# Seven block products in place of eight for the values of blocks 0 and 1, made between two down products

## The reference

```python
qkv = x @ w_qkv.T                                  # 512 -> 3 * 512
q, k, v = ...                                      # 16 heads of 32
q = q * cos + rotate_half(q) * sin                 # k likewise
scores = einsum('bhqd,bhkd->bhqk', q, k) * scale   # keep 0 <= q - k < 64
attn = softmax(scores); out = einsum('bhqk,bhkd->bhqd', attn, v)
x = layernorm(x + out @ w_out.T)
gate = silu((x @ w_gate) * s_gate); up = (x @ w_up) * s_up
x = layernorm(x + ((gate * up) @ w_down) * s_down)
```

## Time and profile before

| what | value |
| --- | --- |
| time, median of 3 runs | 1167.76 us (1167.47 to 1167.96) |
| time of the profiled execution | 1167.22 us |
| its span | 1165.4 us |
| busy: PE, DVE | 1154.4 us (99%), 985.7 us (85%) |
| busy: POOL, ACT | 587.9 us (50%), 584.5 us (50%) |
| granted PE clock, mean | 0.999 of full speed |

### The profile page before, as it was taken

How to read it: one execution, slowest core, us unless ns; L and a number is a source line. 1 busy time by engine, 2 the same in 40 slices (tenths; PEclk the granted TensorE clock), 3 DMA queues, 4 the chain that set the end, 5 groups by cost and what they waited for, 6 DMA issues and landing times.

```text
span 1165.4 us, 25537 instructions
## 1 busy us (share of the span) xinstructions
PE 1154.4 (99%) x8433; PEld 569.4 (49%) x8433; DVE 985.7 (85%) x2820; ACT 584.5 (50%) x1640; POOL 587.9 (50%) x563
## 2 busy tenths in 40 slices
PE   9999999999999999999999999999999999999997
PEld 4344446444464444644455444554445544464444
DVE  7899998898988989879998899897898988986434
ACT  3863883048820588105880159701686027950330
POOL 0775684256731667326671367613676236752330
PEclk9999999999999999999999999999999999999999
DMA  9999786356662665617656086561964527734000
GB/s 296 164 182 244 140 170 152 71 88 137 115 149 55 108 130 110 144 42 128 130 99 141 37 146 119 100 132 42 159 124 87 131 64 137 119 73 109 19 1 36
DMA packets 351933, 134.80 MB, mean 116 GB/s; under 512 B 309824, under 2 KB 332224, under 8 KB 351808
## 3 DMA queue, kind: packets, MB, share of 16 engines
q1 hardware_dynamic: 334832, 106.73, 49.2%
q0 software_dynamic: 10560, 17.30, 5.0%
q10 hardware_dynamic: 6416, 9.13, 2.1%
HBM read 32.19 MB, written 8.39 MB: 35 GB/s over the span
## 4 chain that ended last, share of the span: by engine, by line
PE 96%; ACT 1%; DVE 1%; issue 1%; POOL 0%; POOLq 0%
PE bank L835 61%; PE bank L1051 18%; PE bank L841 10%; PE bank L977 3%; PE bank L957 2%; PE bank L857 1%; ACT bank L1236 1%; PE bank L1073 1%; PE bank L866 0%; PE bank L1062 0%; ACT wu L1179 0%; DVE fuse L1364 0%; ACT fuse L1179 0%; PE bank L941 0%; DVE row_max L1536 0%
## 5 line engine op out<-in xcount | busy, mean ns | idle before, releaser
L835 PE MATMUL bank<-x1T,wg 128*128 128x512 f16 (+1 forms) x1032 | 242.5, 378 | 0.0
L835 PE MATMUL bank<-x1T,wu 128*128 128x512 f16 x1024 | 241.9, 379 | 0.0
L1236 ACT ACTIVATE bank<-bank,neg_max,qk_scale 128x128 f32<-128x128 f32 x512 | 220.7, 436 | 8.1 <-DVE neg_max L1549 6.2
L1051 PE MATMUL bank<-wd,fuse 128*128 128x512 f16 (+1 forms) x1056 | 222.7, 373 | 0.0
L653 POOL TENSOR_TENSOR fuse<-ffn_tmp,fuse 128x512 f16<-128x512 f32 x128 | 149.8, 1170 | 117.0 <-ACT fuse L1179 116.4
L735 POOL TENSOR_TENSOR fuse<-fuse 128x512 f16<-128x512 f32 x116 | 137.6, 1218 | 74.0 <-ACT fuse L1179 71.9
L1051 PEld LDWEIGHTS bank<-wd,fuse 128*128 128x128 f16 x1056 | 103.1, 98 | 116.6 <-DVE y L1604 0.2
L835 PEld LDWEIGHTS bank<-x1T,wu 128*128 128x128 f16 x1024 | 100.2, 98 | 120.6
L648 POOL TENSOR_TENSOR xT_sb<-probs,xT_sb 128x512 f16<-128x512 f32 x112 | 129.9, 1160 | 44.6 <-ACT xT_sb L1179 44.5
L835 PEld LDWEIGHTS bank<-x1T,wg 128*128 128x128 f16 x1032 | 96.4, 98 | 113.9 <-issue 4.0
L1189 ACT ACTIVATE ffn_tmp<-bank,tanh_scale 128x512 f32<-128x512 f32 x128 | 88.3, 690 | 99.5 <-PE bank L835 74.9
(11 more groups left out here) (234 smaller groups left out, 1624.6 us busy)
## 6 DMA issues: line engine op xcount, KB each, us to landing
v_cross<-v_own SPq DMA_DIRECT2D x64, 128.0 KB, 2.4
out<-x ACTq DMA_DIRECT2D x32, 256.0 KB, 2.0
xT_sb<-xT SPq DMA_DIRECT2D x30, 256.0 KB, 4.0
qkT<-x SPq DMA_DIRECT2D x28, 256.0 KB, 3.7
wg<-w_gate POOLq DMA_DIRECT2D x7, 1024.0 KB, 5.1
wu<-w_up POOLq DMA_DIRECT2D x7, 512.0 KB, 5.9
wqkv<-w_qkvT SPq DMA_DIRECT2D x8, 256.0 KB, 6.0
wg<-w_gate POOLq DMA_DIRECT2D x1, 2048.0 KB, 8.2
```

The costliest lines, as they stand in the source:

```text
L835: last = pe.matmul(dst, lhsT, rhs, start=(i == 0), stop=(i == len(pairs) - 1))
L1051: last = pe.matmul(dst[:, cols], fuse[:, s, z, rows], wd[:, s, cols], start=(s == 0 and z == 0), stop=(s == STEPS - 1 and z == 1))
L1236: last = act.activation(unit, unit, ACT.Exp, bias=neg_max[:, s % 2, h // 3, h % 3:h % 3 + 1], scale=qk_scale[:, 2:3], accum_out=row_sum[:, ...
```

## The change

The values of blocks 0 and 1 of the next tile are made by `project_v_pair` with seven block products of 128 rows by 256 columns in place of eight, and PE runs it between down products 2 and 3. The sums of weights for it are made by POOL in each body (`add_v_weights`), after it has inverted the first layer norm's deviations; POOL's reload of the gate and up columns, which it overwrites, moves behind the values. ACT keeps the first product (`keep_v_first`) between the stores of rows 0 and 1. DVE sums the products (`sum_v`, seven additions of 256 columns) ahead of `finish_y(f, 2)` and keeps the low halves (`split_v_pair`). The rope sums of blocks 0 and 1 go from DVE to POOL. `carry_keys` and `start_tables` move ahead of `start_y(f, 1)`.

```diff
+            def add_v_weights(a):
+                low_left, low_right, high_left, high_right = v_quarters()
+                wait(proj_done, pool, a - 1, NB - 1)
+                done(v_weights_added, pool.tensor_tensor(added_out(2), high_right, low_right, ALU.subtract))
+                wait(v_weights_added, pool, a - 2, 0)
+                done(v_weights_added, pool.tensor_tensor(added_out(1), added_out(2), low_left, ALU.add))
...
                 if more:
+                    rope_sums(a + 1, 0, ffn)
                     split_low(a + 1, 0, ffn)
+                    rope_sums(a + 1, 1, ffn)
...
+            def project_v_pair(a):
...
+                wait(proj_read, pe, a - 1, NB - 1)
+                done(v_product, quarter(front_left, front_low, low_left))
+                wait(x_summed, pe, a - 1, 3)
+                wait(v_weights_added, pe, a - 2, 3)
+                done(v_product, quarter(back_right, sums[:, 2, :, :], added_out(2)))
+                wait(v_first_kept, pe, a - 2, 0)
+                done(v_product, quarter(front_left, front_high, high_left))
+                done(v_product, quarter(back_left, sums[:, 1, :, :], added_out(1)))
+                done(v_product, quarter(front_right, sums[:, 0, :, :], added_out(0)))
+                wait(v_summed, pe, a - 2, V_SUM_SECOND)
+                done(v_product, quarter(back_left, back_high, added_out(3)))
+                wait(v_summed, pe, a - 2, V_SUM_FOURTH)
+                done(v_done, quarter(front_right, sums[:, 3, :, :], high_right), 2)
...
                 if attn:
-                    project_v(a, 1, ffn)
                     project_v(a, 2, ffn)
                     scores(a, 0, ffn)
                     scores(a, 1, ffn)
...
+                    if more and j == 2:
+                        project_v_pair(a + 1)
                 if more:
                     for i in range(2):
                         project_pair(a + 1, i)
-                    project_v(a + 1, 0, ffn)
...
+            def keep_v_first(a):
+                wait(v_product, act, a - 2, O_FIRST)
+                wait(ln2_chain, act, a - 2, 4 * 1)
+                done(v_first_kept, copy(v_kept_products()[0], v_places()[0]))
...
                 for j in range(NB):
+                    if more and j == 1:
+                        keep_v_first(a + 1)
                     if more and j == 2:
+                        keep_v_pair(a + 1)
+                    if more and j == NB - 1:
                         keep_first(a + 1, 0)
                     wait(y_ready, act, f, j)
                     dst = out[bass.ds(f * TILE + j * P, P), :]
                     act.dma_start(dst, x1[:, j, :]).then_inc(y_moved[j], 16)
...
                 rope_products(a, 2 * i, True, range(2, 4), paired=True)
-                rope_sums(a, 2 * i, True)
-                if i == 0:
+                if i:
+                    wait(rope_done, dve, a, 1)
+                    rope_sums(a, 2 * i, True)
+                else:
                     sum_back_even(a, i)
...
                 if more:
                     sum_x(a + 1, f)
                     next_scales(a, ffn)
+                    carry_keys(a + 1)
+                    start_tables(a + 1)
                 for j in range(1, NB - 1):
                     start_y(f, j)
                     finish_y(f, j - 1)
+                if more:
+                    sum_v(a + 1, range(7))
```

More of the change, by code:

```diff
@@ L810, in body @@
                         invert_deviation1(a, j)
-                        if j == 1:
-                            reload_columns(a)
+                        if j == 1 and not more:
+                            reload_columns(a, more)
+                    if more:
+                        add_v_weights(a + 1)
                 for j in range(NB):
@@ L1209, in keep_v, with keep_v_pair @@
                                   v_scale[:, 1:2]))
+            def keep_v_first(a):
+                wait(v_product, act, a - 2, O_FIRST)
+                wait(ln2_chain, act, a - 2, 4 * 1)
+                done(v_first_kept, copy(v_kept_products()[0], v_places()[0]))
+            def keep_v_pair(a):
+                wait(proj_done, act, a - 1, 1)
+                for place, half, summed in V_HALVES:
+                    wait(v_summed, act, a - 2, summed)
+                    heads = slice(half * HEADS // 2, (half + 1) * HEADS // 2)
+                    last = copy(v_own[:, place // 2, heads, 0, :], v_places()[place].rearrange("p (h d) -> p h d", d=HEAD_DIM),
+                                v_scale[:, 1:2])
+                    if half:
+                        done(v_high, last)
             def carry_v(a):
@@ L1282, in first @@
                     split_x1_high(a, j, ffn)
+                for j in range(2):
+                    keep_v(a + 1, j, True)
             def body(t, attn, ffn, more):
@@ new lines, in split_v_pair @@
+            def split_v_pair(a):
+                for place, half, summed in V_HALVES:
+                    j = place // 2
+                    heads = slice(half * HEADS // 2, (half + 1) * HEADS // 2)
+                    wait(v_high, dve, a, j)
+                    last = dve.scalar_tensor_tensor(out=v_own[:, j, heads, 1, :],
+                                                    in0=v_places()[place].rearrange("p (h d) -> p h d", d=HEAD_DIM),
+                                                    scalar=v_scale[:, 1:2], in1=v_own[:, j, heads, 0, :],
+                                                    op0=ALU.mult, op1=ALU.subtract)
+                    if half:
+                        done(v_low, last)
@@ L1795, in first @@
                 rope_sums(a + 1, NB - 1, True)
+                for j in range(2):
+                    split_v(a + 1, j, True)
             def front(t, more, attn=True):
@@ L1799, in front @@
                 if attn:
-                    for j in range(2):
-                        split_v(a, j, ffn)
                     for s in range(2):
@@ L1862, in front @@
                     finish_y(f, j - 1)
+                if more:
+                    sum_v(a + 1, range(7))
             def back(t, more):
                 a, f, ffn = t, t - 1, True
+                finish_y(f, NB - 2)
+                if more:
+                    split_v_pair(a + 1)
                 start_y(f, NB - 1)
-                finish_y(f, NB - 2)
                 if more:
@@ L1870, in back @@
                     sum_fourth(a + 1, 0)
-                    carry_keys(a + 1)
-                    start_tables(a + 1)
                 finish_y(f, NB - 1)
```

69 lines of the change are left out of this document (62 added, 7 removed).

## The result

The changed kernel takes 1239.97 us (median of 5 runs, 1238.65 to 1240.85), the kernel before 1167.47 beside it: ratio 1.0617, 95% interval 1.0606 to 1.0629. It is slower, as forecast, but by 72 us where 43 were forecast and 60 were the end of the range.

The account below looks back on a forecast made before the run. PE, busy for all 141.92 us of a period, was taken to bound the kernel. -0.87 + 2.9 + 4.3 + 0.9 = +7.2 us a tile, six times +43.4 on 1167.22, forecast 1211 us; range 1186 to 1228.

Parts of the forecast that it names:

- the three waits: PE's waits a tile: inside the value products 2.9 us, at scores 1 4.3 us, at the second gate product 0.9 us.
- the clock: Rival, chance 0.13: PE falls to 1.2 GHz after the wait at scores 1, up to 3.5 us a tile, 1232.
- step 4: Second gate product: PE waits for the low half of block 3's values, 0.9 us a tile (bounds 0 and 1.4).
- Step 1: Values of blocks 0 and 1 on PE: seven block products take 6.06 us for 6.93, saving 0.87 us a tile.
- Step 2: Inside the value products: PE waits for ACT's copy of the first product, 2.9 us a tile (bounds 1.0 and 3.8).
- Step 3: Scores 1: PE waits until block 3's rope products are read, 4.3 us a tile (bounds 2.1 and 4.9).
- Step 5: DVE's seven value sums and four splits, and POOL's later column reload: costed at nothing.
- The bounds: Sums of the waits' limits with the saving: +13 us (1181) by the lower, +55 us (1223) by the upper.

Follow-up runs that it names:

- three mends: The changed kernel with kept products in unused v_own rows, block 3's values ahead of the scores, and DVE beginning result block 0 earlier: 1204.1 us.
- values_left_out: The kernel before, value products of blocks 0 and 1 left out from the second tile on but for one small product each (values wrong): 1156.0 us.
- ropes_back_on_vector: The changed kernel with the rope sums of blocks 0 and 1 back on DVE: 1232.5 us, ratio 1.0568.
- filled_waits: The changed kernel with products that serve nothing put into PE's waits inside the value pair and ahead of scores 0 and 1: 1246.0 us.
- ropes_alone: The kernel before with only the rope sums of blocks 0 and 1 moved to GpSimd: 1170.2 us, ratio 1.0034.

## Why the prediction was right and wrong

The direction, the places of the three waits and their releasers were right. The sum was 4.5 us a tile short: 2.4 in A, where the clock and a fourth wait, at down product 2, stood at nothing, and 2.1 in B, where step 4 had the wrong link.

- **Step 1, right in size.** Seven products cost 6.06 (A with three mends). What I did not see is that the 6.93 taken out of B had a second bound beneath them: only 1.9 of them could come back (values_left_out), and in the changed kernel none did (B 42.61 for 42.25).
- **Step 2, right, with some luck in the number.** 2.67 for 2.9 in the row, 3.0 in A. The blocking was two full waits: a scaling that the step had not counted took 1.49 for 0.54 and ended 0.3 after POOL's first sum, and the two splits of x1 took 2.36 for 1.47 beside POOL's last. With 0.1 at the other scaling they made `start_y(f, 0)` 2.2 later, for the 1.9 taken, and the tables another 1.0, for 0.82. `finish_y(f, 0)` was so 3.2 later, 3.01 from the start of `start_y(f, 1)` to its end as before; but PE was itself 0.6 late by then, by down product 2. DVE's timeline before, which stands ahead of the earlier trace rows:

```profile
488.36 0.54 DVE L1591 TENSOR_SCALAR qkT<-qkT,mean_var,rstd 128x512 f32<-128x512 f32 x1
```

and after, DVE and then POOL:

```profile
669.11 1.49 DVE L1722 TENSOR_SCALAR qkT<-qkT,mean_var,rstd 128x512 f32<-128x512 f32 x1
...
673.28 2.36 DVE L1727 SCALAR_TENSOR_TENSOR qkT<-qkT 128x512 f16<-128x512 f32 x2
...
683.65 0.69 DVE L1735 TENSOR_TENSOR y<-bank,sdown 128x512 f32<-128x512 f32 x1
...
686.12 0.54 DVE L1769 TENSOR_SCALAR x<-x,mean_var,rstd 128x512 f32<-128x512 f32 x1
```

```profile
668.95 1.37 POOL L733 TENSOR_TENSOR wu<-wqkv 128x512 f32<-128x512 f32 x1
...
673.03 1.45 POOL L738 TENSOR_TENSOR wg<-wqkv 128x512 f32<-128x512 f32 x1
```

- **Step 3, right in time, by a neighbouring path.** Block 3's rope products ended at T' + 31.66 (729.88 + 2.47) for 32.0, and scores 1 started at 31.7 in every period: 4.0 us after PE could have (27.7), for 4.3. A part of it, 1.1 to 1.7 in five of the six periods, is spent at scores 0 on the transposes of block 0. But the step let DVE start these products only once POOL's low parts of block 1 were done, at + 29.5. They were done at + 28.7, and DVE started at + 29.2, straight from block 2's rope sums, which took 3.0 beside POOL's low parts where 1.2 would do. So DVE's own chain, put at + 29.8 by the step, with 1.8 of blocking is what ended last here, half a microsecond behind the path that the step took. The rope sums of block 2:

```profile
726.91 1.48 DVE L1458 TENSOR_TENSOR fuse<-fuse 128x512 f32<-128x512 f32 x1
728.32 1.63 DVE L1459 TENSOR_TENSOR fuse<-fuse 128x512 f32<-128x512 f32 x1
```

- **Step 4 failed.** It reads: "Now: block 3 read at + 32.0, its rope sums 2.7, 0.2, 5.62: + 40.5". The rope sums ended at + 34.5, near the 34.7 of that sum. But ACT's high halves did not follow them by 0.2: they waited for block 1's transposes until + 37.4. The same 5.6 behind that gives + 43.0, and 43.09 was measured (42.6 in most periods). In the kernel before, ACT came to the high halves of block 3 at T + 35.2, straight from the copy of block 2's values and without a wait. PE's own values had held ACT up to there, not the rope sums (done at 542.50, T + 33.7) and not the transposes:

```profile
543.43 0.69 ACT L1179 ACTIVATE v_own<-bank,v_scale 128x512 f16<-128x512 f32 x1 [2.81 <-PE bank L841]
544.01 2.17 ACT L1179 ACTIVATE fuse<-fuse 128x512 f16<-128x512 f32 x4
```

With less of PE's work ahead of that copy the transposes came next, at T + 34.56 in values_left_out. I took the length of the chain from its last link on, not from what could hold the link. This is the 2.1 of B. How much of it is POOL's is seen from three kernels, by the medians of when ACT went on and of B: + 34.7 and 40.37 in values_left_out, + 35.9 and 41.60 in ropes_back_on_vector, + 36.9 and 42.61 in the change. The low half of block 1 ended at + 27.3 in the first two, as before, and at + 28.7 in the change. So the rope sums on POOL are 1.0 of it. The 1.2 between the first two lie in the transposes themselves, and what makes them land later stays open; in the last two periods of ropes_back_on_vector they do not (+ 34.6 and + 34.4, B 40.3).

- **Step 5 failed by what it left out.** For what it names no wait of PE is seen, but the step left out down product 2, which waits 0.6 us for `start_y(f, 0)` behind the same late splits. Removing it gave 0.76 (34.50 to 33.74).
- **The clock, a rival at 0.13,** came in both waits. It was priced at scores 1, where it costs nothing, since the chain of step 4 covers slow products there (filled_waits), and not in the value pair, where nothing covers it: 1.5 us a tile. Its 1232 comes near for the wrong place. The 2.4 in A are these 1.5, 0.76 for down product 2 and 0.1 by which step 2 was short (3.0 for 2.9).
- **The bounds** were bounds of each wait. They left out the clock in A and the wrong link in B, so the range ended too low. The span adds up: the six periods grew by 68.1 us together where 43.4 were forecast, and the first down product of these periods starts 3.3 later, which the prediction had costed at nothing with the end of tile 0 (2.7 of it are the rope sums, ropes_alone): 71.4.

No version that leaves nothing out beats the kernel before. With A mended, its 33.74 and B's 36 make 0.2 us less than before, and C gives back 5.9. Whether the softmax chain can be shortened by those 5.9 stays open; the two orders that I tried only moved the wait on.

## What to carry to other kernels

An engine that is busy all the time can still stand right above a second chain. Before taking work out of a stretch, follow each semaphore at its end back through the other engines and find when it would come if this engine were never late; only the difference is there to be gained. To test it, leave the work out of the kernel before and see how much time comes back. And follow each link by what its instruction waits for, buffers that it overwrites too, not by the gap that the trace shows ahead of it.

Slow products behind a wait are not a cost until something waits for them: fill the wait and look whether the end of the stretch moves.

## What I had not expected of the hardware

The clock fell to half after PE had stood for 2.67 us between dense products, and the next four records took 2.08 us for 1.03; in the fifth period it did not after 2.68 us (1.13). In values_left_out, with waits of 0.53 and 1.95 us around the scores, the mean granted clock of the profiled execution was 1.000; in the three others it was 0.989, 0.999 and 0.995.

DVE stood for whole additions of POOL, as in tile 0. The scaling at 669.11 went on only when POOL's sum of 668.95 had ended (1.49 for 0.54), and the two splits at 673.28 took 0.9 more than their 1.47 beside the sum that POOL ran from 673.03 to 674.48. The reduction between them, in which DVE reads 2048 elements, took 2.28 beside POOL's sums and 2.28 before without them.
